# A differential-attention layer with a ternary feed-forward part: the feed-forward cycle shifted by half a block, one gelu for a pair of row tiles, two-part fp16 scores

## The reference

```
x = x + attention(layernorm(x))          # x: (8, 1024, 512) fp32
x = x + ffn(layernorm(x))

# attention: 32 query heads and 16 key heads of width 16, in pairs (1, 2); 8 value heads of width 32
q, k = rope(q), rope(k);  q *= 16 ** -0.5
p = softmax(q @ k.T + causal)
diff = p[head pair, 0] - lambda * p[head pair, 1]
attn = rmsnorm(diff @ v) * subln_weight * (1 - lambda_init);  return attn @ Wo.T

# ffn: w1 (2048, 512) and w2 (512, 2048) quantised to -1, 0, 1
h = gelu(x @ w1q.T + b1);  return h @ w2q.T + b2
```

## Time and profile before

| | us |
|---|---|
| median of three runs (lowest, highest) | 4375.46 (4370.62, 4382.93) |
| the profiled execution | 4370.7 |
| its span in the trace | 4368.9 |
| from the span's start to the first exponential | 87.8 |
| from the last exponential to the span's end | 95.6 |
| mean granted PE clock | 0.90 of full speed |

### The profile page before, as it was taken

How to read it: one execution, slowest core, us unless ns; L and a number is a source line. 1 busy time by engine, 2 the same in 40 slices (tenths; PEclk the granted TensorE clock), 3 DMA queues, 4 the chain that set the end, 5 groups by cost and what they waited for, 6 DMA issues and landing times.

```text
span 4368.9 us, 81035 instructions
## 1 busy us (share of the span) xinstructions
PE 3625.1 (83%) x23454; PEld 2157.1 (49%) x23454; DVE 3369.0 (77%) x6188; ACT 2913.5 (67%) x6786; POOL 1495.9 (34%) x1563
## 2 busy tenths in 40 slices
PE   2688888888888888888888988888888888888886
PEld 1345554455445454554545545555545555554553
DVE  6778967888678886788767887678877788678881
ACT  1567766777567775677756766667666777567772
POOL 0243234332333334332343324433134432333323
PEclk7788999989899899998889988999989989899998
DMA  4212112211122112212122110222122111222110
GB/s 133 54 25 41 24 43 43 40 23 33 35 43 43 23 38 46 43 25 38 26 43 43 36 31 23 47 37 43 25 44 43 32 31 25 44 43 43 20 37 14
DMA packets 146768, 166.71 MB, mean 38 GB/s; under 512 B 16640, under 2 KB 117632, under 8 KB 145792
## 3 DMA queue, kind: packets, MB, share of 16 engines
q1 hardware_dynamic: 146304, 161.13, 18.3%
HBM read 105.95 MB, written 55.12 MB: 37 GB/s over the span
## 4 chain that ended last, share of the span: by engine, by line
PE 41%; DVE 25%; issue 19%; ACT 8%; DMA 3%; SPq 2%; POOL 1%; DVEq 1%; ACTq 1%; POOLq 0%
DVE NM L667 9%; PE M L822 7%; PE M L872 7%; PE SP_ L837 6%; PE F L894 6%; PE DP L849 5%; PE F L907 4%; DVE E L691 3%; ACT E L543 3%; DVE CC L688 2%; DMA KST<-scratch 2%; PE M L816 2%; DVE NM L675 2%; PE SP_ L838 1%; PE DX L849 1%
## 5 line engine op out<-in xcount | busy, mean ns | idle before, releaser
L543 ACT ACTIVATE E<-SP_,NM 128x256 f32<-128x256 f32 (+7 forms) x2048 | 1518.3, 743 | 674.7 <-DVE NM L667 461.8
L667 DVE TENSOR_REDUCE NM<-SP_ 128x1 f32<-128x896 f32 (+3 forms) x1024 | 1034.2, 1018 | 257.8 <-PE SP_ L838 254.0
L837 PE MATMUL SP_<-KST,QST 96*128 96x512 bf16 (+3 forms) x3072 | 866.2, 356 | 394.5 <-ACT E L543 329.5
L691 DVE SCALAR_TENSOR_TENSOR E<-E,CC 128x512 f32<-128x512 f32 (+7 forms) x1024 | 928.6, 907 | 36.2
L555 ACT ACTIVATE DT<-DP 128x512 f32<-128x512 f32 (+3 forms) x1024 | 527.7, 515 | 534.9 <-PE DP L849 501.5
L849 PE MATMUL DP<-ident,E 128*128 128x128 f32 x3328 | 617.5, 304 | 140.4 <-DVE E L691 136.7
L675 DVE TENSOR_REDUCE NM<-SP_ 128x2 f32<-128x1024 f32 (+3 forms) x512 | 420.2, 821 | 309.2 <-PE SP_ L838 306.5
L837 PEld LDWEIGHTS SP_<-KST,QST 96*128 96x128 bf16 x3072 | 278.9, 103 | 745.7 <-ACT E L543 515.0
L894 PE MATMUL F<-X2H,W1Q 128*128 128x256 f16 x2048 | 512.1, 287 | 71.0 <-ACT HP L598 67.0
L849 PEld LDWEIGHTS DP<-ident,E 128*128 128x128 f32 x3328 | 395.6, 154 | 313.9 <-issue 164.3
L822 PE MATMUL M<-WQKV,WT 128*128 128x512 f32 x1040 | 531.7, 608 | 8.8 <-DVE T L650 4.1
(11 more groups left out here) (87 smaller groups left out, 4794.6 us busy)
## 6 DMA issues: line engine op xcount, KB each, us to landing
QST<-scratch SPq DMA_DIRECT2D x390, 128.0 KB, 4.4
scratch<-SPL SPq DMA_DIRECT2D x65, 576.0 KB, 2.8
KST<-scratch SPq DMA_DIRECT2D x390, 64.0 KB, 4.8
X<-in_x SPq DMA_DIRECT2D x66, 256.0 KB, 3.3
out<-SQ SPq DMA_DIRECT2D x64, 256.0 KB, 2.0
KST<-in_w1T SPq DMA_DIRECT2D x1, 4096.0 KB, 19.4
DT<-in_w2T SPq DMA_DIRECT2D x1, 4096.0 KB, 28.8
WQKV<-in_wqT SPq DMA_DIRECT2D x1, 1024.0 KB, 6.9
```

The lines of the kernel that those rows point to most:

```text
L543: act.activation(dst, score_out(i, 2 * n + k, w), ACT.Exp, bias=NM[:, (2 * u + k) % 8:(2 * u + k) % 8 + 1], scale=1.0, accum_out=SUM[:, i ...
L667: nc.vector.tensor_reduce(NM[:, m:m + 1], score_out(i, 2 * n + k, P * (i + 1)), AX.X, ALU.max, negate=True).then_inc(max_ready, 1)
L691: nc.vector.scalar_tensor_tensor(out=E1[:, u % 2, 0:w], in0=E2[:, e:e + w], scalar=CC[:, u % 2:u % 2 + 1], in1=E1[:, u % 2, 0:w], op0=ALU. ...
L837: pe.matmul(SP_[:, k[a // 512], 0:n], q, KST[0:ROWS, a // P:(a + n) // P, kk, :], start=True, stop=not last)
```

## The change

1. **The cycle of the feed-forward part** is shifted by half a block. The first product's chunks 0 to 4 run in odd blocks at half-steps 15 to 28, chunks 5 to 7 in the next even block at 1 to 8. One gelu over all 4096 columns follows ACT's half-step 10 of the even block. POOL's eight hidden splits stand at half-steps 11 to 18 of the same block. The second product runs in eleven half-steps instead of thirteen: row tile 0 at 19 to 29 of the even block, row tile 1 at 1 to 11 of the next odd block; the outputs are at 31 and 13. It may begin once the first hidden splits are there, not only after the eighth.
2. **No scaling pass**: POOL's L462 is gone, and the output is a plain sum.
3. **Two-part fp16 scores on shared rows**: a score is three products of 16 rows instead of six. Two key heads share the 96 rows; the query rows of the other are zero, set once. The parts are fp16: the high part (ACT), the rest times 64, and the high part over 64 (both POOL, now two one-input passes without a wait between). The matmuls keep their count and shape. The stacking copies keep their count (3 parts for each of 2 halves, for Q and K); each moves half the bytes, in pieces half as long.
4. **The second exponential row twice**: `E2` has two full rows, so the second exponential of a pair waits for the combination two pairs back instead of one.
5. The ternary weights are read by four loads, reduced and cut in four parts, since the key buffer has halved. Four blocks instead of three follow the attention.

```diff
@@ the constants
-PROD = 6
-QPART = (0, 0, 0, 1, 1, 2)
-KPART = (0, 1, 2, 0, 1, 0)
-ROWS = PROD * DH
-GELU_F = FT // 2
+PROD = 3
+QPART = (0, 2, 1)
+KPART = (0, 1, 2)
+PART = PROD * DH
+ROWS = 2 * PART
+LOW = 64.0
-W1_AT = (1, 4, 7, 10, 13, 16, 19, 22)
-GELU = (13, 25)
-SPLIT_AT = (14, 16, 17, 18, 26, 27, 28, 29)
-W2_AT, W2_N = (3, 18), 13
-OUT_AT = (17, 31)
+W1_ODD, W1_EVEN = (15, 18, 21, 24, 27), (1, 4, 7)
+GELU = 10
+SPLIT_AT = (11, 12, 13, 14, 15, 16, 17, 18)
+W2_ODD, W2_EVEN, W2_N = 1, 19, 11
+OUT_ODD, OUT_EVEN = 13, 31
@@ stack, SP
-                for j in range(PROD):
-                    sp.dma_start(QST[DH * j:DH * (j + 1), tile % 2, :, :].rearrange("p (s c) n -> p s c n", s=8),
-                                 src[QPART[j], :, :, 0:4, :]).then_inc(stacked, 16)
+                for a in range(2):
+                    for j in range(PROD):
+                        r = PART * a + DH * j
+                        sp.dma_start(QST[r:r + DH, tile % 2, :, :].rearrange("p (s c) n -> p s c n", s=8)[:, :, 2 * a:2 * a + 2, :],
+                                     src[QPART[j], :, :, 2 * a:2 * a + 2, :]).then_inc(stacked, 16)
@@ split and hidden_split, POOL
-                pool.tensor_scalar(SPL[:, 1, c], T2[:, c], 1.0, 0.0, ALU.mult, ALU.add).then_inc(mid_part, 1)
-                after(pool, mid_part, 2 * nb + part + 1)
-                pool.tensor_tensor(SPL[:, 2, c], T2[:, c], SPL[:, 1, c], ALU.subtract).then_inc(split_done, 1)
+                pool.tensor_scalar(SPL[:, 1, c], T2[:, c], LOW, 0.0, ALU.mult, ALU.add)
+                pool.tensor_scalar(SPL[:, 2, c], SPL[:, 0, c], 1.0 / LOW, 0.0, ALU.mult, ALU.add).then_inc(split_done, 1)
-                after(pool, gelu_done, 2 * q + k // 4 + 1)
+                after(pool, gelu_done, q + 1)
                 hold(pool, f2_ready, 2 * q)
-                hold(pool, h_chain, 2 * n + 1)
-                pool.tensor_scalar(HP[:, h, :], HP[:, h, :], HS, 0.0, ALU.mult, ALU.add).then_inc(h_chain, 1)
@@ exp, ACT
-                    after(act, d_ready, b * N_U + u - (1 if i < 4 and u > 0 else 0))
-                    e = 512 * (u % 2) if i < 4 else 0
-                    dst = E2[:, e:e + w]
+                    after(act, d_ready, b * N_U + u - 1)
+                    dst = E2[:, u % 2, 0:w]
@@ act_work
-                    if T.w1 and hs in GELU:
-                        j = GELU.index(hs)
-                        after(act, hp_ready, 8 * T.pair + 4 * j + 4)
+                    if T.w1 and not T.odd and hs == GELU:
+                        after(act, hp_ready, 8 * T.pair + 8)
                         act.activation(HP[:, :, :], HP[:, :, :], ACT.Gelu).then_inc(gelu_done, 1)
@@ second_product, PE
                 if fs[0] == 0:
-                    hold(pe, h_ready, 8 * q + 8)
                     hold(pe, hp_ready, 8 * q + 8)
                     hold(pe, o_sum, 2 * q + j)
+                hold(pe, h_ready, 8 * q + fs[-1] // 2 + 1)
```

151 lines of the change are left out of this document (80 added, 71 removed).

## The result

The changed kernel is slower. Its median is 4442.1 us (lowest 4440.0, highest 4443.4, four runs) against 4373.0 for the kernel before on the same chip (4364.0 to 4382.9, four runs): ratio 1.0159, 95% interval 1.0139 to 1.0178. The forecast was 4369 us, its range ended at 4410, and slower had a chance of 0.32.

A forecast was written before the change was run, and what follows sets the result against it. DVE was fullest in wide blocks; engine-to-engine chains set narrow ones, and gelu stalls lengthened odd blocks. Terms -15 - 27 + 40 - 7 + 0 - 10 + 13 = -6 on the median 4375.5 gave 4369 us, 8-in-10 range 4305 to 4410.

The forecast's parts named there:

- the stall in block 2: Seven pairs' gelus move to block 2, each an uncovered stall of 1.7 plus 1.7 us: +24 us.
- a relief of 10 us beside the projections: Fewer feed-forward pieces of PE beside the projections, for which DVE waits 94.6 us: -10 us, bounds 0 and -40.
- Block 0, +40: End of block 0: gelu, POOL's splits, keys' split and copies end 5.7 us later, seven times: +40 us.
- One gelu for two, wide, -15: Wide blocks: 4.3 us uncovered stall instead of 5.25, 16 pairs at 0.95 us: -15 us, bounds 0 and -43.
- The rival of the whole gain: Wide pairs save 2.7 us each (-43) and the projections' relief is 40: 4311 us; chance 0.35.
- Narrow blocks, -27: 15 pairs' gelus leave blocks 1 and 3 at 3.4 us each (-51), seven go to block 2 (+24): -27 us.
- The new scores: Halved key copies: 7 x 2.4 us in block 0 and 7 at the batch boundary, 24 us faster.
- the -7: Batch boundary, seven times: half the bytes take 1 us off PE's wait for key copies: -7 us, bounds 0 and -14.
- The clock rival: Even blocks: PE at half clock behind the new gelu, 1.5 us a pair, +45: 4414 us; chance 0.29 with a longer block 0.
- the second row and the scaling pass at nothing: Doubled row in blocks 4 to 7: wait ends no earlier, 0; scaling pass, 0.70 us of each split, has no own term.
- the end at +13: Behind the last exponential, more chunks, gelu and splits stick out by 12 us, last pair +1: +13 us, bounds 5 and 20.
- The three signs of being wrong: Block 0 not longer, a batch's wide blocks over 8 us shorter together, or even blocks' granted clock down a tenth.

The follow-up runs named there:

- j_noscale_e2: Kernel before with the new scores, no scaling pass and the second exponential's row twice, feed-forward cycle unshifted: 4334.8 us, ratio 0.9897.
- n_two_gelus: Changed kernel with two gelus of 2048 columns, at half-step 27 of the odd and 10 of the even block: 4444.0 us, ratio 1.0156.
- h_late_pieces: Changed kernel with even blocks' first-product pieces at half-steps 3, 6, 9, gelu at 12, hidden splits at 13 to 20: 4453.7 us, ratio 1.0178.
- m_filler_nogelu: Changed kernel, gelu replaced by a one-column copy, plus three unread 512-column products in each of half-steps 11 to 18 of even blocks: 4244.0 us, ratio 0.9701.
- d_gelu11: Changed kernel with the gelu one half-step later, at 11 instead of 10: 4430.7 us, ratio 1.0125.
- e_short_low: Changed kernel with the low part of each hidden split over 32 of its 256 columns, so POOL ends earlier: 4428.9 us, ratio 1.0118.
- b_after_nogelu: Changed kernel with its gelu, and so the table loads, replaced by a copy of one column: 4283.9 us, ratio 0.9790.
- l_fill: `j_noscale_e2` plus twelve unread 128-column products in each half-step 25 to 31 of blocks 5, 7 and 0 to 2 of 4, 6: 4282.6 us, ratio 0.9770.
- i_noscale: Kernel before with the new scores and without the pass that scales the hidden values: 4327.3 us, ratio 0.9883.
- The two mends: Changed kernel with pieces, gelu and splits two half-steps later in blocks 0, 2 and unread filler products in 4, 6: 4411.4 us, ratio 1.0064.

## Why the prediction was wrong

The mechanisms of single steps mostly held; the sum did not, because one thing that moved had no price.

- **The step that failed: what the move of PE's work costs in the even blocks.** The prediction gave the even blocks their price in two terms, the chain over POOL (+40, all of it in block 0) and the stall in block 2 (+24 for seven), and took PE's FFN work itself as free, even as a relief of 10 us beside the projections. That relief did not come (DVE waits 93.9 us for them in place of 94.6), and the shift measured +113 us (`j_noscale_e2` to `n_two_gelus`), 17.2 a batch. The runs show three costs in it, each found in a kernel of its own. The pieces at half-steps 1 to 8 stand ahead of the narrow blocks' scores and cost 3.4 and 2.3 us a batch in half-steps 0 to 9 (`h_late_pieces`). The stretch from half-step 11 to 18, with no FFN work, runs partly at half clock and costs 2.2 and 2.6 us in blocks 4 and 6 even without a gelu (`m_filler_nogelu`). And the gelu at half-step 10 splits a pair, which costs two to three microseconds in each narrow block (`d_gelu11`); all in all a pair's one gelu costs 4.9 us in the new cycle where its two cost 3.6 in the old.
- **Block 0, +40.** It got longer, by 8.8 us a batch, more than the 5.7 forecast, and the times of the chain were right within a microsecond. The cause was wrong: 8.1 of the 8.8 us lie in half-steps 0 to 19, ahead of the chain's end, and a chain 3.3 us shorter gave back 1.2 us (`e_short_low`). The chain is close behind, though: it becomes the bound as soon as the pieces or the gelu's place are mended (waits of 4.10 and 5.24 us in `h_late_pieces` and `d_gelu11`), which is why single mends give so little in this block. That the forecast had the right sign here, and a size near it, is luck.
- **One gelu for two, wide, -15.** Right in kind, mis-sized: DVE waits 5.01 us (plus 1.21 at the next scores) in place of 5.25, and the wide blocks gain 1.1 us a batch, 8 us in all. A removed gelu takes its cover with it. The rival of the whole gain (4311) falls with this.
- **Narrow blocks, -27.** Wrong. Leaving out all gelus of the kernel before shortened its blocks 1 and 3 by 2.3 and 0.6 us only, so a pair that leaves them was worth that and not 3.4. Of the excess of block 1, the upper bound, half stays with the gelus gone (5.6 us over the mean of its neighbours, 2.7 without them; means of batches 1 to 6); what it is was not taken apart, the first product stands there. In the new cycle a gelu in a narrow even block costs 2.7 and 4.9 us (`b_after_nogelu`).
- **The new scores.** Mis-sized in the other direction: 50 us in place of 24. The wait for the copies in block 0 went (17.5 us in all), and PE spends 116 us less at half clock. At the batch boundary nothing was gained, against the -7: PE waits 3.88 us there (3.04 in the earlier trace rows). Halving the bytes did not bring the six key copies forward there. Before, and then after:

```profile
2158.55 3.94 SPq L389 DMA_DIRECT2D KST<-scratch  x6
...
2180.97 3.65 SPq L404 DMA_DIRECT2D KST<-scratch  x6
```

  Issuing them takes 3.94 and 3.65 us, and the score comes 5.8 us behind the first issue before (2164.35) and 6.6 after (2187.54).
- **The clock rival** (4414) named a mechanism that the runs show, and the measured time lies 28 us beyond it. It counted one low stretch behind the gelu; there are two in each wide even block. Its counterweight, that the old low stretch behind half-step 25 goes away, came true and was worth nothing to be seen: with a filler there blocks 5 and 7 get no shorter (`l_fill`). But the clock alone does not make the loss (at most 34 of the 113 us of the shift). The Trainium skill (TensorE: Matmul & The Clock Gate, the part on the clock gate) says that the default is throttled and activity releases it; the runs agree, 24 further products bring 0.84 to 1.00 in the windows above.
- **Right:** the second row and the scaling pass at nothing (`j_noscale_e2`, `i_noscale`), the end at +13 (measured 106.6 - 95.6 = +11.0), the gelu of 3.7 us (3.62), no drain behind a table load (3.62 us of gelu start 1.29 us after the load's start). The three signs of being wrong did not help: block 0 is longer, the wide blocks of a batch are not shorter but 3.6 us longer together, and the even blocks' clock fell by 0.06 and 0.04 in blocks 0 and 4, not by a tenth.
- **Pieces of 256 B.** The key copies land in 1.9 us (median of 390) where pieces of 512 B landed in 4.8. By the Trainium skill's rule (DMA: Bandwidth & Descriptors, Specifications) the key half should have gained nothing; the trace does not agree. But it does not measure the rule either: before, the key copies ran behind the query copies on full DMA engines, and the quickest of them landed in 2.1 us, after the change in 1.7.

Open stays how the 113 us divide exactly. The three costs come to about 15 of the 17.2 us a batch, but they were measured in different kernels and need not add up. The two mends together return about 31 to 42 us; the filler's own work and the chain over GpSimd take part of what they give. The interplay of the gelu with the key projections behind it was not taken apart.

## What to carry to other kernels

When work is moved, price the place that it leaves as well as the place that it goes to: the stretch without it may run at half clock, and in a narrow block it may stand ahead of the chain that feeds everything. An engine that interrupts its stream is covered up to the work queued on its neighbours, so one long interruption was no cheaper here than two short ones that each have cover. When two chains end close together, mending one shows little; look at what the other's wait became. And before an edit is bundled, time its parts alone: here one part (the scores, 0.9891) was hidden by another.

## What the runs showed of the hardware that was not expected

- Added work made the kernel faster. Twelve 128-column products, whose result nothing reads, in each of ten half-steps of the pairs in wide blocks took 1.0 to 1.3% off the time, as the granted clock went up (0.69 to 1.00 in the window of block 6).
- Half clock has no fixed price. At the end of blocks 5 and 7 some 15 us of it a batch could be taken away without a gain (`l_fill`), while in the middle of blocks 4 and 6 removing 16 us made them 4.8 us shorter there (`m_filler_nogelu`).
- Two table loads of 1.28 us, added to the pass of 3.6 us between them, cost more than the pass by itself: 105 against 56 us over 32 gelus. Behind pass and loads half clock was 41.3 us a batch, behind the pass alone 19.5.
- The clock fell also away from the gelu: the third of the four windows of the kernel after has PE busy for 5.3 of 6.8 us at a clock of 1.00, and the fourth runs at 0.50.
- Copies whose bytes and pieces were halved (256 B) landed in 1.9 in place of 4.8 us where they had run behind others, while at the batch boundary, where no query copies run ahead of them, the last of them came no sooner: PE waits 3.88 us in place of 3.04.
